# A Macaron layer on one core: router logits without transposes back, fillers set by VectorE and POOL, W1 loaded behind the token stores

## The reference, cut to what matters

```python
x = x + 0.5 * ffn(layernorm(x))     # 8 experts, 128 -> 512 -> 128
x = x + attn(layernorm(x))          # 16 heads of 8
x = x + 0.5 * ffn(layernorm(x))     # the same weights

def ffn(x):
    indices = argmax(softmax(x @ Wr + br))         # Wr is 128 x 8
    for i in range(8):
        xi = x * (indices == i)
        out += relu(xi @ W1[i] + b1[i]) @ W2[i] + b2[i]
```

## Time and profile before

| | us |
|---|---|
| median of 3 runs | 998.96 |
| lowest, highest | 998.92, 1000.32 |
| profiled execution, its own time | 1000.25 |
| span of the profiled execution, first to last instruction | 998.4 |
| mean granted TensorE clock | 0.968 of full |
| busy: PE, DVE, ACT, POOL | 918.1, 829.9, 752.1, 217.3 |

### The profile page before, as it was taken

How to read it: one execution, slowest core, us unless ns; L and a number is a source line. 1 busy time by engine, 2 the same in 40 slices (tenths; PEclk the granted TensorE clock), 3 DMA queues, 4 the chain that set the end, 5 groups by cost and what they waited for, 6 DMA issues and landing times. The chain is left out here.

```text
span 998.4 us, 17986 instructions
## 1 busy us (share of the span) xinstructions
PE 918.1 (92%) x5975; PEld 382.3 (38%) x5975; DVE 829.9 (83%) x1396; ACT 752.1 (75%) x1509; POOL 217.3 (22%) x315
## 2 busy tenths in 40 slices
PE   3789966889999999999999999999999999965996
PEld 2689853422222222222222222222222222434996
DVE  6766558979999999999999999999999998768664
ACT  3367636878888888888888888888888888754774
POOL 5157631841000001000000100000100000024775
PEclk9789988989999999999999999999999999996998
DMA  8624535842220203202022120220202000051321
GB/s 265 184 86 120 160 108 191 257 168 63 63 60 17 62 30 85 61 18 62 15 72 75 31 62 15 72 54 28 75 30 64 30 22 17 1 170 48 104 64 43
DMA packets 68130, 78.67 MB, mean 79 GB/s; under 512 B 13088, under 2 KB 45512, under 8 KB 68040
## 3 DMA queue, kind: packets, MB, share of 16 engines
q1 hardware_dynamic: 61464, 64.52, 22.2%
q0 software_dynamic: 5120, 12.59, 4.1%
q10 hardware_dynamic: 1456, 0.41, 0.2%
HBM read 40.47 MB, written 33.49 MB: 74 GB/s over the span
## 5 line engine op out<-in xcount | busy, mean ns | idle before, releaser
L1561 DVE TENSOR_REDUCE maxima<-ps_m 128x2 f32<-128x1024 f32 x512 | 602.6, 1220 | 58.2 <-PE ps_m L1324 56.3
L1531 ACT ACTIVATE probs<-ps_s 128x512 f32<-128x512 f32 x1024 | 555.9, 599 | 109.1 <-PE ps_s L1370 78.7
L1370 PE MATMUL ps_s<-q,k 74*128 74x512 bf16 (+1 forms) x1024 | 312.1, 386 | 3.0 <-ACT probs L1531 3.0
L1381 PE MATMUL ps_o<-probs,vs 128*32 128x512 f32 x2048 | 273.6, 606 | 0.7 <-ACT probs L1531 0.7
L1370 PEld LDWEIGHTS ps_s<-q,k 74*128 74x128 bf16 (+1 forms) x1024 | 79.6, 97 | 307.1 <-ACT probs L1531 219.1
L1324 PE MATMUL ps_m<-k,q 64*128 64x512 bf16 x1024 | 160.1, 386 | 5.1 <-DVE maxima L1561 4.0
L1254 POOL TENSOR_SCALAR split<-top 128x16 bf16<-128x16 f32 x32 | 8.1, 253 | 443.0 <-DVE top L1577 429.3
L690 PE MATMUL ps_y<-W,hT 128*128 x624 | 86.4, 281 | 3.4 <-DVE hT L846 2.1
L1324 PEld LDWEIGHTS ps_m<-k,q 64*128 64x128 bf16 x1024 | 48.9, 93 | 102.3 <-issue 57.0
L1381 PEld LDWEIGHTS ps_o<-probs,vs 128*32 128x32 f32 x2048 | 40.3, 108 | 109.7 <-issue 94.7
L690 PEld LDWEIGHTS ps_y<-W,hT 128*128 128x128 f32 x624 | 78.1, 195 | 5.3 <-issue 5.1
(11 more groups left out here) (213 smaller groups left out, 571.7 us busy)
## 6 DMA issues: line engine op xcount, KB each, us to landing
k_rows<-parts SPq DMA_DIRECT2D x24, 384.0 KB, 4.4
sums<-oT SPq DMA_DIRECT2D x30, 256.0 KB, 2.1
q<-q_parts SPq DMA_DIRECT2D x75, 96.0 KB
k<-k_rows SPq DMA_DIRECT2D x15, 288.0 KB
token_rows<-x SPq DMA_DIRECT2D x16, 256.0 KB, 3.8
token_rows<-v_and_ctx SPq DMA_DIRECT2D x16, 256.0 KB, 4.1
k<-k_rows SPq DMA_DIRECT2D x15, 256.0 KB
q_parts<-parts SPq DMA_DIRECT2D x8, 384.0 KB, 3.4
```

Source lines behind the costliest of these rows:

```text
L1370: nc.tensor.matmul(ps_s[n % 3][:, :], k2[buffer(g)][0:contracted, j, kt * P:(kt + 1) * P], q2[buffer(g)][0:contracted, j, u * HALF:(u + 1) ...
L1381: last = nc.tensor.matmul(ps_o[32 * j:32 * (j + 1), :], vs[buffer(g)][:, kt, j, :], probs[:, s % 2, j, :], start=(kt == 0), stop=(kt == KT ...
L1531: nc.scalar.activation(probs[:, s % 2, j, :], ps_s[n % 3][:, :], ACT.Exp, scale=SCALE).then_inc(exped, 1)
L1561: nc.vector.tensor_reduce(maxima[:, :, pr, qt, kh], ps_m[slot][:, :, :], AX.X, ALU.max).then_inc(unit_free[slot], 1)
```

## The change

Three parts.

1. Router logits, in both routings. `Route.logits` now runs once per quad: the turned tokens are the stationary operand (128x128), `Wr` the moving one with 8 columns, and the result stands with tokens on partitions, so that `copied_logits` and `turn_logits` go. PE's order is turn 0, turn 1, then logits q and turn q + 2. `Wr` loses its padding, DVE reads the logits contiguously. In the front, ACT normalises quads 0, 1, 2 before it copies, POOL 3 and 6, DVE 4, 5 and 7 (before: ACT 0, 2, 7; POOL 1, 3, 5; DVE 4, 6), and PE's wait for the small loads moves behind the second turn.
2. Fillers. `sync_fill` and its twelve transfers go; DVE sets the ones of `k2` by six memsets behind its last result of the first expert stage, POOL the zeros of `q2` and the ones of `vs` by six memsets behind its last scatter. SP waits for `filled` in front of the first query load. `blank` and half of `units` go, with their memsets.
3. SP issues the load of W1 behind the sixteen token stores.

```diff
-        sp.dma_start(w["W1"][:, :, 0:HID], dram["L0_ffn_W1"].rearrange("e d h -> d e h")).then_inc(self.w1_load, 16)
+
+    def sync_weights(self, sp):
+        sp.dma_start(self.w["W1"][:, :, 0:HID], self.dram["L0_ffn_W1"].rearrange("e d h -> d e h")).then_inc(self.w1_load, 16)
...
-        nc.gpsimd.memset(self.blank[:, 0, :], 0.0).then_inc(self.made, 1)
-        nc.gpsimd.memset(self.blank[:, 1, :], 1.0).then_inc(self.made, 1)
...
-        sp.wait_ge(self.made, 12)
-        for p in range(BUFS):
-            sp.dma_start(self.k2[p][64:96, 0::2, :], constant(1, slice(64, 96))).then_inc(self.filled, 16)
-            sp.dma_start(self.k2[p][0:64, 1::2, :], constant(1, slice(0, 64))).then_inc(self.filled, 16)
-            sp.dma_start(self.q2[p][0:64, 1::2, :], constant(0, slice(0, 64))).then_inc(self.filled, 16)
-            sp.dma_start(self.vs[p][:, :, :, :].rearrange("p t j c -> p (t j c)").rearrange("p (a c) -> p a c", c=2 * P),
-                         self.units[:, :].unsqueeze(1).to_broadcast([P, KT * GH * 32 // (2 * P), 2 * P])).then_inc(self.filled, 16)
+    FILLED = 4 * BUFS
+    def vector_fill(self):
+        for p in range(BUFS):
+            for tile, rows, first, value in ((self.k2[p], slice(64, 96), 0, self.PAIR), (self.k2[p], slice(0, 64), 1, self.PAIR)):
+                self.nc.vector.memset(tile[rows, first::2, :].bitcast(F32), value).then_inc(self.filled, 1)
+    def gpsimd_fill(self):
+        for p in range(BUFS):
+            self.nc.gpsimd.memset(self.q2[p][0:64, 1::2, :].bitcast(F32), 0.0).then_inc(self.filled, 1)
+            self.nc.gpsimd.memset(self.vs[p][:, :, :, :], 1.0).then_inc(self.filled, 1)
...
-    def logits(self, pe, h):
-        pe.wait_ge(self.t_out, QUAD * (h + 1))
-        wait_unless_zero(pe, self.lT_out, h)
-        for j in range(QUAD):
-            last = self.nc.tensor.matmul(self.ps_lT[32 * j:32 * (j + 1), :], self.w["Wr"][:, :], self.xnT[:, QUAD * h + j, :], start=True, stop=True)
-        last.then_inc(self.lT_full, 1)
-    def turn_logits(self, pe, h):
-        pe.wait_ge(self.lT_out, h + 1)
-        for i in range(QUAD):
-            last = self.nc.tensor.transpose(self.ps_l[h][:, i * P:(i + 1) * P], self.logitT[:, h, i * P:(i + 1) * P], self.w["ident"][:, :])
-        last.then_inc(self.l_full, 1)
+    def logits(self, pe, q):
+        pe.wait_ge(self.t_out, q + 1)
+        for i in range(QUAD):
+            place = (q % QUAD * QUAD + i) * EXPERTS
+            last = self.nc.tensor.matmul(self.ps_l[q // QUAD][:, place:place + EXPERTS], self.xnT[:, q, i * P:(i + 1) * P], self.w["Wr"][:, :], start=True, stop=True)
+        if q % QUAD == QUAD - 1:
+            last.then_inc(self.l_full, 1)
...
-    BY_ACT, BY_POOL = (0, 2, QUADS - 1), (1, 3, QUAD + 1)
+    BY_ACT, BY_POOL = (0, 1, 2), (3, QUAD + 2)
...
-        for q in range(QUAD + 1):
-            turn(q)
-        self.route.logits(pe, 0)
-        turn(QUAD + 1)
-        self.route.turn_logits(pe, 0)
-        for q in range(QUAD + 2, QUADS):
-            turn(q)
-        self.route.logits(pe, 1)
-        self.route.turn_logits(pe, 1)
+        for q in range(2):
+            turn(q)
+        self.setup.small_loaded(pe)
+        for q in range(QUADS):
+            self.route.logits(pe, q)
+            if q + 2 < QUADS:
+                turn(q + 2)
```

More of the change, by code:

```diff
@@ L291, with __init__ @@
     UNIT = float(2 ** 23)
-    def __init__(self, nc, memory, semaphores, w, dram, tag, xn_sb, routes, ps_t, ps_lT, ps_l, ps_r, ps_f, xnT, logitT, columns, marks):
+    def __init__(self, nc, memory, semaphores, w, dram, tag, xn_sb, routes, ps_t, ps_l, ps_r, ps_f, xnT, columns, marks):
         def sb2(name, shape, dt):
@@ L362, in copied @@
         self.nc.scalar.activation(self.xnT[:, q, :], self.ps_t[q % 2][:, :], ACT.Copy).then_inc(self.t_out, 1)
-    def copied_logits(self, act, h):
-        act.wait_ge(self.lT_full, h + 1)
-        self.nc.scalar.activation(self.logitT[:, h, :], self.ps_lT[:, :], ACT.Copy).then_inc(self.lT_out, 1)
     def mark(self, act):
@@ L382, in choose @@
         dve.wait_ge(self.l_full, h + 1)
-        nc.vector.tensor_tensor(logit.rearrange("p (j i) e -> p j i e", i=QUAD),
-                                self.ps_l[h].rearrange("p (i j e) -> p j i e", i=QUAD, j=QUAD)[:, :, :, 0:EXPERTS],
-                                self.w["br"][:, :].unsqueeze(1).unsqueeze(1).to_broadcast([P, QUAD, QUAD, EXPERTS]), ALU.add).then_inc(routed, 1)
+        nc.vector.tensor_tensor(logit, self.ps_l[h][:, 0:half * EXPERTS].rearrange("p (t e) -> p t e", e=EXPERTS),
+                                self.w["br"][:, :].unsqueeze(1).to_broadcast([P, half, EXPERTS]), ALU.add).then_inc(routed, 1)
         dve.wait_ge(routed, done + 1)
@@ L556, in sync @@
             self.route.store(sp, q, 0, self.xn_sb)
+        self.setup.sync_weights(sp)
         sp.wait_ge(self.route.stored, 2 * 16 * QUADS)
@@ L1183, in _ @@
                     sp.wait_ge(tiles.x_in[r], 16 * (TILES // LANDING))
-                tiles.setup.sync_fill(sp)
-                sp.wait_ge(tiles.setup.filled, tiles.setup.FILLED)
                 tiles.stored(sp)
@@ L1190, in _ @@
                 store(0)
+                sp.wait_ge(tiles.setup.filled, tiles.setup.FILLED)
                 first_load(0)
@@ L1272, in _ @@
                 tiles.gpsimd(pool)
+                tiles.setup.gpsimd_fill()
                 tiles.setup.small_loaded(pool)
@@ L1438, in _ @@
                     do_unit(kind, MERGED)
-                for q in range(QUAD):
+                for q in range(2):
                     turn_next(q)
-                route.logits(pe, 0)
-                turn_next(QUAD)
-                route.turn_logits(pe, 0)
-                for q in range(QUAD + 1, QUADS):
-                    turn_next(q)
-                pe.wait_ge(unit_free[free], freed + 1)
-                route.logits(pe, 1)
-                route.turn_logits(pe, 1)
+                for q in range(QUADS):
+                    if q == QUAD:
+                        pe.wait_ge(unit_free[free], freed + 1)
+                    route.logits(pe, q)
+                    if q + 2 < QUADS:
+                        turn_next(q + 2)
                 route.count(pe)
@@ L1676, in _ @@
                 tiles.vector(dve)
+                tiles.setup.vector_fill()
                 for q in range(FIRST):
```

40 lines of the change are left out of this document (14 added, 26 removed).

## The result

The changed kernel took 1002.62 us (median of 14 executions, 1000.62 to 1010.48), the kernel before 999.5 beside it (14, 997.44 to 1000.32): a ratio of 1.0045, 95% interval 1.0029 to 1.0061. Slower by 0.45%: 3.1 us between the medians, 4.5 us by the ratio. The profiled execution took 1006.53 us for a span of 1004.6, 3.9 us above its own median, so its trace shows more loss than the typical execution has. How that comes is part of what follows.

What follows compares the result with a forecast made beforehand. TensorE leads and bounds the first expert stage, which filler transfers slow. Stall -5.7, fills +0.4, front +6.9 and second routing +5.6 sum to +7.2: 1007.4 us profiled, 1006.2 as median, range 992 to 1010.

Steps and rivals of the forecast that it cites:

- rival B: Only the front is cold and the second routing keeps its clock: +1.7, 1000.7 us; chance 0.17.
- The front, +6.9: First routing's logits: 88 steps at half clock from 18.85, ending at 37.8 where VectorE began at 30.97: +6.9 us.
- The pair at the two levels: One weight load with its 8-column matmul in the logits: 0.11 us at full clock, 0.21 at half.
- The second routing, +5.6: Second routing's logits: +0.1 us at full clock, but the clock falls at 889 and the rest runs at half speed: +5.6.
- the forecast's case: Cold front and a clock that falls in the second routing: own range 1001.5 to 1010 us; chance 0.45.
- The stall, -5.7: First expert stage: without filler transfers, six items taking 17.09 us return to 1.90 each: -5.7 us.
- POOL's bound of 5.95: First expert stage: POOL's 31 further scatters at 1.29 each let the last start at 131.5, not 137.45, allowing 5.95 us.
- VectorE's fills, +0.4: Behind the first expert stage: VectorE's six memsets take 5.7 to 6.5 us, 0 to +0.5 over its idle time: +0.4.
- the cover of 6.03: VectorE's 6.03 us idle after its last first-expert-stage result, until the tokens land, expected to hide most of its six memsets.
- C: Weight loads keep TensorE's clock up as matmuls do, full clock in both routings: -7.4, 991.6 us; chance 0.30.
- D: Logits pairs don't overlap and take 0.30 us each: +24 on C, 1016 us; chance 0.03.
- E: Saturated DMA engines didn't stall TensorE, so 5.7 isn't won: 1011.9 with the forecast's case, 997.3 with C; chance 0.05.

Runs made afterwards that it cites:

- e2_logits_alone: The changed kernel with the fillers back as transfers and W1 back early, leaving only the new logits: 1063.82 us, ratio 1.0089 to the kernel before.
- e1b_fillers_again: The kernel before with only the fills moved to VectorE and POOL, in the changed kernel's order, timed again on the third chip: 997.87 us, ratio 0.9976.
- e3_w1_alone: The kernel before with only the load of W1 moved behind the token stores: 1055.45 us, ratio 1.0001.
- e9_wide_second: The changed kernel with router weights padded by zero columns to 128 in the second routing alone: 1002.3 us, ratio 1.0015 to the kernel before.
- e4b_wide128_again: The changed kernel with router weights padded by zero columns to 128 in both routings, timed again on the third chip: 996.32 us, ratio 0.9959 to the kernel before.
- c1_changed_again: The changed kernel unaltered, measured and profiled once more: 1001.47 us, ratio 1.0033 to the kernel before.
- e5_narrow_warm: The changed kernel, still 8 columns, with extra transposes keeping TensorE turning before its first logits: 997.41 us, ratio 0.9979 to the kernel before.
- e7_fillers_grouped: The kernel before with the fills on VectorE and POOL, VectorE's fills of the same partitions behind one another: 993.95 us, ratio 0.9943.
- e6_wide_warm: The changed kernel padded to 128 columns, with extra transposes keeping TensorE turning before its first logits: 995.45 us, ratio 0.9951 to the kernel before.
- e1_fillers_alone: The kernel before with only the fills moved to VectorE and POOL, timed on the first chip: 1053.97 us, ratio 1.0009.

## Why the prediction was right

**Direction and sign.** Forecast 1006.2 in 992 to 1010, measured 1002.6; a change of +7.2 was forecast, +3.1 to +4.5 measured. The mechanism held for the front, which loses to the clock in every profile, and for the stall that goes; the second routing loses in some executions only. `e2_logits_alone`, `e1b_fillers_again` and `e3_w1_alone` give the signs part by part: +9 us, -2, 0.

That the time lay inside is in part the width of the range, 18 us, which holds rival B's 1000.7 as well; 1002.6 is nearer to B than to the forecast. And that the first profile gives +6.2 where the sum has +7.2 is in part luck: the attention's +1.35, in no term, made up for much of what the second routing lacked.

**The front, +6.9.** Measured 6.6 in both profiles of the changed kernel; against the same profile of before, the other fronts of 8 columns from cold give 6.4 (`e2_logits_alone`) and 7.0 (`e9_wide_second`). Start at 18.85 (19.27), 88 steps of 0.213 (a group of 12 in 2.45 is 0.204), reader at 37.8 (37.58), clock 0.50 throughout: each step of the sum is in the trace. Half clock throughout was my estimate: no row of before shows 8-column pairs, or what the clock does under them. The changed kernel has 0.50 in every window of 2 us from 18 to 38. Its reason is shown by the runs: with 128 columns instead of 8, nothing else changed, 7.2 us come back; and with a warm start and 8 columns, 8.1.

**The pair at the two levels.** I took 0.11 and 0.21 from the earlier trace rows. The changed kernel has 2.45 us a group of twelve steps at half clock (0.204 a step) and 1.28 at full (0.107), and eight pairs of it take 1.71 and 0.96. One weight load of the logits has a median of 333 ns in this front, at 0.50, and of 192 in that of `e4b_wide128_again`, most of it at 1.00. With 0.11 a pair at both levels the front would have ended near 31.2 (18.85 + 64 x 0.11 + 24 x 0.213 + 0.2), and it ended at 37.58.

**The second routing, +5.6.** This is the term that was mis-sized. The step that failed is "in the find stage it fell some 3 us after its first weight load", from which I took the fall at 889, 4 us into the logits. The row was read wrongly: I took TensorE as busy there, but in the window before the fall it was busy 1.17 us of 2, while the logits leave no gap. It fell 6 us in (+3.2), or 9 us in, with the last pairs (+0.5 in `e2_logits_alone`, +0.3 in `c1_changed_again`). With the transposes between the products the second routing lasts 10 us, and in `e5_narrow_warm` such a stretch, begun warm, held the clock for 9. I had that argument ("transposes recur there every quad") in rival B and gave it 0.17. B was worth about as much as the forecast: the forecast's case and B's, 1000.7, are both there, as the profiles at 1006.53 and 1000.58. That it is the transposes that hold the clock so long is argued, not shown, for no run left them out.

**The stall, -5.7.** Measured 5.9, with items at 1.90 us (94.07 to 113.03, ten items) and a last scatter 5.94 earlier relative to the first gather, POOL's bound of 5.95; and 7.3 in the second profile. The bound held only as long as the first scatter stood where it had: in `c1_changed_again` it came 44.4 us after the first gather, not 46.0. Why it came earlier there was not found.

**VectorE's fills, +0.4.** The spill past the tokens' landing is 0.7 (143.52 to 144.22). One fill is busy 0.91, less than the 1.07 that I took (the +0.4 and the cover of 6.03 over six; four times the 0.27 of 256 elements was the bound), but 0.27 stands before each: the pitch is 1.18. I priced the instruction and not the gap. The fills of POOL, 139.09 to 144.53, and W1 cost nothing that the stretches show, as forecast.

**Not in the sum: the attention, +1.35** in the first profile, 0.0 in the second. In the windows of its first 40 us the clock rises and falls at other times in each execution: it first rises at 146 before, and near 153 in both profiles of the changed kernel, of which one has the 1.35 and the other nothing. So the later rise alone isn't it. The same stretch, whose code no kernel here changes, lasts 708.5 us before, 707.3 in `e7_fillers_grouped`, 707.4 in `e9_wide_second`, and 709.8 in the first profile and in `e5_narrow_warm`. So it varies by 2.5 us between executions, and 1.35 need not be the change's at all; what makes it vary was not found.

**The rivals.** C (weight loads keep the clock up) is refuted by `e5_narrow_warm` beside `e6_wide_warm` (0.50 and 1.00 from 28 to 30) and by the front of every 8-column kernel begun cold (0.50 from 36 to 38 in the changed kernel and in `e2_logits_alone`); the kernel nearest to what C assumes, `e6_wide_warm`, takes 995.5, not 991.6. Its front gains 2.0 against before, near C's 2.2, and its first gather to last scatter 6.8; its profile gives this back in the attention (+1.1) and in the second routing (+2.8, the clock that fell before it), and 0.95 goes to the fills. One sum on C was loose: 5.3 us of loss in both routings makes the kernel equal to before, and for a time below 997 it must be less than 3.3. D: pairs stand 0.12 apart (0.96 for eight), not 0.30. E: with the transfers gone, the stall is gone (TensorE at 4.00 of 4 us from 100 to 104, where it had 2.83).

**Left open.** Why the medians of the filler kernels differ by 3 us where their order explains 0.4, and why fronts of the same code differ by 1.7. Why more executions of the changed kernel than of the kernel before are 3 us and more above the lowest: the clock is lower in them (0.950 to 0.952 against 0.952 to 0.961 in `c1_changed_again`), and one profile of each group differs in the second routing and in the attention, but which of these makes the group, no run decides.

## What to carry to other kernels

Few moving columns were cheap here by their own duration (eight pairs in 0.96 us, against 1.06 with 128 columns) and dear by the clock: 8 columns under a 128x128 weight load, begun cold, lost 7 us in 18. Padding them with zeros won it back for 0.05 us a group of eight pairs, and so did keeping TensorE busy ahead of them. So before TensorE gets work that streams less, look at the granted clock in the windows ahead of it, and at whether it begins cold. And take a bundle of edits apart before keeping it: the fills alone beat both kernels (ratio 0.9976 in the bundle's order, 0.9943 and 993.95 us grouped), and the bundle hid that behind its logits.

## What the runs showed of the hardware that was not expected

- VectorE idles 0.27 us before a memset whose partitions differ from the one before, and 0.16 where they are the same (`e7_fillers_grouped`); POOL's memsets of the same size follow each other every 0.89 us.
- On the first of the three chips the kernel before takes 1054.7 us and not 1000. The 50 us lie in the two expert stages: the first one, from first gather to last result, takes 113.8 us in `e1_fillers_alone` and 83.6 in the same kernel on the third chip, and from the second half of the second logits to the end it is 132.7 against 103.8, while the front is the same to 0.7 us. ScalarE and VectorE stand still together for up to 10 us, with the DMA engines hardly busy (0.10 in the window shown), so it isn't the saturation of the earlier trace rows. The first row is VectorE's in that kernel, with a releaser that the profile doesn't know; below it is a window of the same wait:

```profile
119.66 0.29 DVE L852 TENSOR_TENSOR y_sum<-ps_y,w1s 128x128 f32<-128x128 f32 x1 [9.37 <-remote]
```

```profile
116.00:118.00 2.00, 0.00 (x0) 0.00 (x0) 0.00 (x0) 0.00 (x0) 1.39 (x3) 0.50 0.10 33
```

  What it is was not found.
- Whether a kernel's TensorE is warm at one place can depend on the execution: the same changed kernel had its second logits in 4.43 and in 7.33 us, with fronts equal to 0.01 us.
- Early in the span the granted clock is shown as 1.00 where TensorE doesn't keep that pace: two windows of `e5_narrow_warm`, in both of which it only transposes, have 11 and 20 transposes in 2 us. The pace of a known instruction says more there than the clock's column.

```profile
12.00:14.00 2.00, 2.00 (x11) 2.00 (x10) 1.83 (x12) 0.55 (x2) 0.48 (x1) 1.00 0.74 263
14.00:16.00 2.00, 2.00 (x20) 2.00 (x19) 1.97 (x21) 2.00 (x6) 2.00 (x4) 1.00 1.04 386
```
